# Attention in a three-stage kernel: values projected into token layout for two heads at once, and units written out

## The chip, the cores and the metric

One core of one Trainium2 chip runs the whole kernel. The metric is device time in microseconds (us) of that core, the median of several executions of the same program. TensorE is called PE in the profile, VectorE DVE, ScalarE ACT, GpSimd POOL; SyncE (SP) issues the DMA transfers. A weight load of TensorE has a row of its own there, PEld.

## The reference

The input x has four batches of 512 tokens with 256 features. Three stages follow one another, each adding to x: a mixture-of-experts stage, attention, and the mixture-of-experts stage again. The change touches attention alone:

```python
x = x + attn(layernorm(x))
# in attn: 16 heads of 128 features
q = x @ Wq + bq;  k = x @ Wk + bk;  v = x @ Wv + bv    # W = codes * scales, one scale for 32 rows
scores = einsum('bqhd,bkhd->bhqk', q, k) / sqrt(128)
attn = softmax(scores);  out = einsum('bhqk,bkhd->bqhd', attn, v)
return out.reshape(B, S, 2048) @ Wo + bo
```

## The kernel before

**Precision.** Every large product is made of three matmuls (`mm3`, lines 1006 to 1010): an operand is held as a high part and a low part in fp32r, and high by high, high by low and low by high are added up in PSUM. ACT writes the high part (a copy out of PSUM that rounds), DVE the low part (PSUM minus the high part, the helper `low`, line 1202, or `low_biased`, line 1206).

**Start of attention.** The layernorm (`norm_vector` and its companions, lines 237 to 316) writes the transposed, normalised activations xT (256 features by 2048 tokens, high and low). DVE normalises (line 264), PE transposes (line 301), ACT and DVE copy out (lines 315 and 273). POOL computes one small power for it (line 289) before anything else.

**Weights.** SP loads the codes and scales of one head at a time: for each of q, k and v one transfer of codes (line 963) and two of scales, each row read 32 times (line 968), then one transfer of codes and one of scales for the output projection (lines 970 and 972), 11 transfers and 1 MB in all. POOL multiplies them (line 984), makes the high part (989) and the low part (991) of `w`, which is double buffered by head. The raw buffers are single: SP waits for the low part before it loads the next head. Between the weights of head 0 and of head 1, POOL adds the output bias to x (line 997).

**Units.** A unit is one batch of one head; there are 64, in the order head, batch. For a unit the kernel needs the transposed queries and keys (`queries`, `keys`, lines 1020 and 1029: 6 matmuls of 512 columns each, into the banks b_p 0 and 1), and the values in token layout. The values are projected transposed (`values`, line 1036: again 6 matmuls of 512 columns), ACT adds the bias on the way to `vT` (line 1141), and PE turns `vT` back by four 128x128 transposes (`turn_values`, line 1040, matmuls of line 1044). ACT (line 1147) and DVE (line 1202) split the result into high and low.

**The order of the work** is written out by hand in `step(u)` for each engine (PE at line 1085, ACT at 1169, DVE at 1232). A step has four parts i = 0 to 3. In part i PE turns block i of the unit's probabilities (`turn_probs`, line 1062, four transposes), makes the scores of query block i of the next unit (`scores`), multiplies block i-1 of the turned probabilities by the values (`probs_values`), and does one piece more: in part 0 half of an output projection (`output`, six matmuls of 256 columns) and the queries two units ahead, in part 1 the keys two units ahead, in part 2 the values one unit ahead and the other half of an output projection, in part 3 `turn_values`; `probs_values` of block 3 ends the step. ACT copies each turned block (line 1161) and then runs the exponentials of the next unit's block i (line 1154); DVE writes the low part of the turned block (line 1202) and then the row maxima of the next unit's scores (line 1217), then the low parts and the additions of the output into x (line 1225). The first transposes of a step wait for all four exponentials of its unit:

```python
if kb == 0:
    pe.wait_ge(q["exp_done"], 4 * u + 4)
```

Units 0 to 3 and 60 to 63 are written out; the 56 between them are seven turns of a loop of eight units (`schedule`, line 945), in which waits are against register values. `apart` (line 61) increments a semaphore that nobody waits for, between a wait and an ACT instruction.

Of the kernel before, what the change touches and what calls it, by code (L numbers as in the profile page):

```python
# [25 lines left out]
P = 128  # L26
# [204 lines left out]
def norm_buffers(m):  # L231
    return dict(stats=m.sb("ln_stats", [P, NT, 6]), mean=m.sb("ln_mean", [P, NT]), var=m.sb("ln_var", [P, NT]),
                tmp=m.sb("ln_tmp", [P, NT]), rstd=m.sb("ln_rstd", [P, NT]),
                xn=[m.sb(f"ln_xn{s}", [P, 2, D]) for s in range(2)])
# [671 lines left out]
def attention(nc, c, a, tag):  # L906
# [4 lines left out]
    with ExitStack() as ctx:  # L911
# [9 lines left out]
        vT = m.sb("vT", [P, S])  # L921
        v = [[m.sb(f"v{k}_{s}", [P, 4, HD], F32R) for k in range(2)] for s in range(2)]
# [12 lines left out]
        sems = ("raw_in w_mul w_hi w_ready bo_added s_done nmax_ready exp_done rinv_ready t_done pt_hi pt_lo pv_done "  # L935
                "q_done q_hi q_lo k_done k_hi k_lo vT_done vT_sb v_done v_hi v_lo o_done o_hi o_lo out_done x_added passed")
        q = {n: m.sem(n) for n in sems.split()}
        block = ctx.enter_context(nc.Block())
        LOADS = 11

        def late(t, n):

            return not isinstance(t, int) or t >= n

        def schedule(eng, step):

            for u in range(4):
                step(u, u)
# [3 lines left out]
            for u in range(60, U):  # L952
                step(u, u)

        def later(u, n):

            return not isinstance(u, int) or u + n < U

        @block.sync
        def _(sp):  # L960
            def load(h):
                for n, name in enumerate(("wq", "wk", "wv")):
                    sp.dma_start(raw_c[:, n, :].rearrange("p (c f) -> p c f", c=DC),
                                 a[name + "_codes"].rearrange("(c p) f -> p c f", p=P)[:, :, bass.ds(h * HD, HD)]
                                 ).then_inc(q["raw_in"], 16)
                    for k in range(DC):
                        rows = a[name + "_scales"][k * (P // BLK):(k + 1) * (P // BLK), bass.ds(h * HD, HD)]
                        sp.dma_start(raw_s[:, n, k * HD:(k + 1) * HD],
                                     rows.unsqueeze(1).broadcast_to([P // BLK, BLK, HD])).then_inc(q["raw_in"], 16)
                sp.dma_start(raw_c[:, 3, :], a["wo_codes"][bass.ds(h * HD, HD), :]).then_inc(q["raw_in"], 16)  # L970
                rows = a["wo_scales"][bass.ds(h * (HD // BLK), HD // BLK), :]
                sp.dma_start(raw_s[:, 3, :], rows.unsqueeze(1).broadcast_to([HD // BLK, BLK, D])).then_inc(q["raw_in"], 16)

            load(0)
            with sp.Fori(1, H) as h:
                sp.wait_ge(q["w_ready"], h)
                load(h)

        @block.gpsimd
        def _(pool):  # L980
            def weights(h, s):

                pool.wait_ge(q["raw_in"], 16 * LOADS * (h + 1))
                pool.tensor_tensor(raw_c[:], raw_c[:], raw_s[:], ALU.mult).then_inc(q["w_mul"], 1)
                pool.wait_ge(q["w_mul"], h + 1)
                if late(h, 2):
                    pool.wait_ge(q["out_done"], 2 * B * (h - 1))
                apart(pool, q["passed"])
                pool.tensor_copy(w[s][0][:], raw_c[:]).then_inc(q["w_hi"], 1)  # L989
                pool.wait_ge(q["w_hi"], h + 1)  # L990
                pool.tensor_tensor(w[s][1][:], raw_c[:], f32(w[s][0][:]), ALU.subtract).then_inc(q["w_ready"], 1)
# [7 lines left out]
            weights(1, 1)  # L999
            with pool.Fori(1, H // 2) as k:  # L1000
                for s in range(2):
                    weights(2 * k + s, s)

        @block.tensor
        def _(pe):
# [6 lines left out]
            def project(bank, n, j):  # L1012

                b0, s = (j % 4) * S, (j // 4) % 2
                for d in range(DC):
                    ins = mm3(bank[:], [t[:, n, d * HD:(d + 1) * HD] for t in w[s]], [t[:, d, b0:b0 + S] for t in xT],
                              d == 0, d == DC - 1)
                return ins

            def queries(u, j, hd):  # L1020
                if j % 4 == 0:
                    pe.wait_ge(q["w_ready"], hd + 1)
                if late(u, 2):
                    pe.wait_ge(q["vT_sb"], u - 1)
                elif u == 1:
                    pe.wait_ge(q["q_lo"], 1)
                project(b_p[0], 0, j).then_inc(q["q_done"], 1)

            def keys(u, j):
                if late(u, 2):  # L1030
                    pe.wait_ge(q["v_lo"], u - 1)
                elif u == 1:
                    pe.wait_ge(q["k_lo"], 1)
                project(b_p[1], 1, j).then_inc(q["k_done"], 1)
# [12 lines left out]
            def scores(u, j, i):  # L1047
# [3 lines left out]
                if late(4 * u + i if isinstance(u, int) else u, 2):  # L1051
                    pe.wait_ge(q["exp_done"], 4 * u + i - 1)
                mm3(b_s[i % 2][:], [t[:, i * P:(i + 1) * P] for t in qT[j % 2]], [t[:] for t in kT[j % 2]],
                    True, True).then_inc(q["s_done"], 1)

            def turn_probs(u, j, kb):
                if kb == 0:
                    pe.wait_ge(q["exp_done"], 4 * u + 4)
                if late(4 * u + kb if isinstance(u, int) else u, 2):
                    pe.wait_ge(q["pt_lo"], 4 * u + kb - 1)  # L1060
                for i in range(4):
                    ins = pe.transpose(b_t[kb % 2][:, i * P:(i + 1) * P], pr[j % 2][:, i, kb * P:(kb + 1) * P],  # L1062
# [3 lines left out]
            def probs_values(u, j, kb):  # L1066
                pe.wait_ge(q["pt_lo"], 4 * u + kb + 1)
                if kb == 0:
                    pe.wait_ge(q["v_lo"], u + 1)
                    pe.wait_ge(q["o_lo"], u)  # L1070
                ins = mm3(b_o[:], [t[:, kb, :] for t in v[j % 2]], [t[:] for t in prT[kb % 2]], kb == 0, kb == 3)
                ins.then_inc(q["pv_done"], 1)

            def output(u, j, o):
# [3 lines left out]
                pe.wait_ge(q["x_added"], 2 * u + o)  # L1078
                for t in range(2):
                    i = 2 * o + t  # L1080
                    ins = mm3(b_out[:, t * D:(t + 1) * D], [z[:, i * P:(i + 1) * P] for z in oT[j % 2]],
                              [z[:, 3, :] for z in w[(j // 4) % 2]], True, True)
                ins.then_inc(q["out_done"], 1)

            def step(u, j):
                for i in range(4):
                    turn_probs(u, j, i)
                    if later(u, 1):
                        scores(u + 1, j + 1, i)
                    if i > 0:  # L1090
                        probs_values(u, j, i - 1)
                    if i == 0 and late(u, 2):
                        output(u - 2, j + 6, 1)
                    if i == 0 and later(u, 2):
                        queries(u + 2, j + 2, (u - j) // 4 + (j + 2) // 4)
                    if i == 1 and later(u, 2):
                        keys(u + 2, j + 2)
                    if i == 2 and later(u, 1):
                        values(u + 1, j + 1)
                    if i == 2 and late(u, 1):  # L1100
                        output(u - 1, j + 7, 0)
                    if i == 3 and later(u, 1):
                        turn_values(u + 1)
                probs_values(u, j, 3)
# [11 lines left out]
            output(U - 2, U - 2, 1)  # L1116
# [191 lines left out]
```

## Time and profile before

| | |
|---|---|
| median of 3 runs | 1524.87 us (1523.44 to 1525.94) |
| span of the profiled execution | 1523.9 us |
| attention, first load issued to last unit's work | about 309 to 1240 us |
| PE, weight loads, DVE, ACT, POOL busy in 500 to 640 us, of 140 us | 138.34, 113.01, 94.45, 83.41, 13.39 us |

The profile is of one execution. Its own time is the span, from the first to the last instruction; the median of the runs is 0.97 us above it. A busy time counts an instruction from its start to its modelled end; matmuls overlap, so the distance between the starts of two matmuls is what one costs, and not its duration.

### The profile page before, as it was taken

How to read it: one execution, taken by the hardware profiler on the slowest of the kernel's cores; microseconds unless marked ns; L12 is line 12 of the kernel's file. 1: busy time of each engine (PE TensorE's matmuls, PEld its weight loads, DVE VectorE, ACT ScalarE, POOL GpSimd, SP SyncE). 2: the span in 40 equal slices, each digit the busy share in tenths (PEclk: the TensorE clock that was granted, in tenths of full speed). 3: DMA queues.
4: the chain of work that ended last, by engine and by line, in shares of the span. 5: the costliest groups of instructions: out<-in, count | busy, mean ns of one | idle time of the engine just before them, and what ended most of it. 6: DMA issues, size and time to landing. Idle time of an engine off the chain costs nothing. (4 is left out here: it accounts for less than half of the span.)

```text
span 1523.9 us, 23702 instructions
## 1 busy us (share of the span) xinstructions
PE 1363.6 (89%) x7023; PEld 1086.8 (71%) x7023; DVE 1024.6 (67%) x2366; ACT 700.9 (46%) x1478; POOL 184.2 (12%) x149
## 2 busy tenths in 40 slices
PE   2887799948999999999999999999999948878998
PEld 1666566836878887888788878888888736665677
DVE  4687466865676667666766676667666766874677
ACT  1432352016566556655655565556555523323510
POOL 1111220042010010101001001001000001112200
PEclk7799899959999999999999999999999968988999
DMA  3100671011010011011001001000000000007701
GB/s 124 39 4 7 172 199 29 0 50 33 1 29 23 6 28 28 0 28 28 4 23 28 13 15 28 18 10 28 22 5 0 1 28 31 7 8 192 200 23 37
DMA packets 98147, 58.94 MB, mean 39 GB/s; under 512 B 42032, under 2 KB 97088, under 8 KB 98112
## 3 DMA queue, kind: packets, MB, share of 16 engines
q1 hardware_dynamic: 96576, 53.26, 12.5%
q0 software_dynamic: 1536, 5.24, 1.8%
q8 instruction: 18, 0.29, 0.1%
q14 instruction: 17, 0.14, 0.0%
HBM read 51.13 MB, written 7.36 MB: 38 GB/s over the span
## 5 line engine op out<-in xcount | busy, mean ns | idle before, releaser
L1202 DVE TENSOR_TENSOR at_prT<-at_b_t,at_prT 128x512 fp32r<-128x512 f32 x256 | 177.1, 692 | 239.2 <-ACT at_prT L1161 232.7
L1154 ACT ACTIVATE at_pr<-at_b_s,at_nmax 128x512 f32<-128x512 f32 x256 | 176.1, 688 | 207.1 <-DVE at_junk L1217 199.8
L1161 ACT ACTIVATE at_prT<-at_b_t 128x512 fp32r<-128x512 f32 x256 | 152.9, 597 | 143.4 <-PE at_b_t L1062 143.3
L1217 DVE TENSOR_SCALAR_CACHE_REDUCE at_junk<-at_b_s 128x512 bf16<-128x512 f32 x256 | 174.2, 681 | 1.3 <-PE at_b_s L1010 1.3
L1062 PE MATMUL at_b_t<-keep_ident,at_pr 128*128 128x128 f32 x1024 | 157.1, 276 | 11.6 <-ACT at_pr L1154 7.3
L1062 PEld LDWEIGHTS at_b_t<-keep_ident,at_pr 128*128 128x128 f32 x1024 | 120.0, 140 | 56.8 <-ACT at_pr L1154 34.7
L1008 PE MATMUL at_b_p<-at_xT,at_w 128*128 128x512 f32 x384 | 152.0, 396 | 1.6 <-DVE at_xT L273 1.5
L1010 PE MATMUL at_b_p<-at_xT,at_w 128*128 128x512 f32 x384 | 152.2, 396 | 0.0
L1009 PE MATMUL at_b_p<-at_xT,at_w 128*128 128x512 f32 x384 | 151.5, 395 | 0.0
L1008 PE MATMUL at_b_s<-at_kT,at_qT 128*128 128x512 f32 x256 | 121.8, 476 | 1.4 <-ACT at_pr L1154 1.4
L1225 DVE SCALAR_TENSOR_TENSOR keep_x<-at_b_out,at_rinv,keep_x 128x256 f32<-128x256 f32 x256 | 111.3, 477 | 2.9 <-PE at_b_out L1010 2.9
L1008 PE MATMUL at_b_o<-at_prT,at_v 128*128 128x512 f32 x256 | 106.0, 414 | 1.9 <-DVE at_prT L1202 1.7
L1010 PE MATMUL at_b_s<-at_kT,at_qT 128*128 128x512 f32 x256 | 101.2, 395 | 0.0
L1010 PE MATMUL at_b_o<-at_prT,at_v 128*128 128x512 f32 x256 | 101.0, 394 | 0.0
L1009 PE MATMUL at_b_s<-at_kT,at_qT 128*128 128x512 f32 x256 | 100.7, 393 | 0.0
L1009 PE MATMUL at_b_o<-at_prT,at_v 128*128 128x512 f32 x256 | 100.1, 391 | 0.0
L1010 PEld LDWEIGHTS at_b_p<-at_xT,at_w 128*128 128x128 f32 x384 | 72.5, 189 | 16.5
L1008 PEld LDWEIGHTS at_b_p<-at_xT,at_w 128*128 128x128 f32 x384 | 72.6, 189 | 16.2 <-DVE at_xT L273 1.9
L1009 PEld LDWEIGHTS at_b_p<-at_xT,at_w 128*128 128x128 f32 x384 | 72.6, 189 | 14.2
L989 POOL CAST at_w<-at_raw_c 128x1024 fp32r<-128x1024 f32 x16 | 16.8, 1052 | 490.8 <-PE at_b_out L1010 490.5
L1008 PE MATMUL at_b_out<-at_w,at_oT 128*128 128x256 f32 x256 | 73.1, 285 | 2.5 <-DVE keep_x L1225 2.5
L745 PE MATMUL e_b_act<-e_guT,e_xgT 128*128 128x512 f32 x128 | 65.8, 638 | 8.8 <-DVE e_guT L847 4.0
(192 smaller groups left out, 2905.1 us busy)
## 6 DMA issues: line engine op xcount, KB each, us to landing
e_raw_g<-in_gate_w SPq DMA_DIRECT2D x32, 256.0 KB, 3.7
e_raw_u<-in_up_w SPq DMA_DIRECT2D x32, 256.0 KB, 3.9
e_raw_d<-in_down_w SPq DMA_DIRECT2D x64, 128.0 KB, 3.9
rows<-f_ln_xn SPq DMA_DIRECT2D x16, 256.0 KB, 2.1
keep_x<-in_x SPq DMA_DIRECT2D x1, 2048.0 KB, 11.9
at_raw_c<-in_wq_codes SPq DMA_DIRECT2D x16, 128.0 KB
at_raw_s<-in_wq_scales SPq DMA_DIRECT2D x32, 64.0 KB
at_raw_c<-in_wk_codes SPq DMA_DIRECT2D x16, 128.0 KB
```

What stands on the lines that cost most here:

```text
L745: ins = pe.matmul(b_act[:], xgT[s][:, k, :], guT[s][:, k, :], start=(k == 0), stop=(k == DC - 1))
L989: pool.tensor_copy(w[s][0][:], raw_c[:]).then_inc(q["w_hi"], 1)
L1008: pe.matmul(out, lhs[0], rhs[0], start=first, stop=False)
L1009: pe.matmul(out, lhs[0], rhs[1], start=False, stop=False)
L1010: return pe.matmul(out, lhs[1], rhs[0], start=False, stop=last)
L1062: ins = pe.transpose(b_t[kb % 2][:, i * P:(i + 1) * P], pr[j % 2][:, i, kb * P:(kb + 1) * P], c["ident"][:])
L1154: act.activation(pr[j % 2][:, i, :], b_s[i % 2][:], ACT.Exp, bias=nmax[:, j % 2, i:i + 1], scale=SCALE, accum_out=rsum[:, j % 2, i:i + 1]) ...
L1161: act.activation(prT[kb % 2][0][:], b_t[kb % 2][:], ACT.Copy).then_inc(q["pt_hi"], 1)
L1202: dve.tensor_tensor(dst, bank, f32(hi), ALU.subtract).then_inc(q[done], 1)
L1217: dve.tensor_scalar(junk[i % 2][:], b_s[i % 2][:], -SCALE, None, ALU.mult, ALU.min, accum_out=nmax[:, j % 2, i:i + 1]).then_inc(q["nmax_re ...
L1225: ins = dve.scalar_tensor_tensor(out=xs, in0=b_out[:, t * D:(t + 1) * D], scalar=rinv[:, j % 4, i:i + 1], in1=xs, op0=ALU.mult, op1=ALU.add)
```

## The change

The units are ordered head pair, batch, head: unit u belongs to pair u // 8, batch (u % 8) // 2, head 2 * pair + u % 2. Weights are loaded, multiplied and split per pair of heads in two parts of 1 MB each: q and k of both heads, then v and the output weights of both heads; each is six transfers, and the second waits until POOL has finished the first. The first queries wait for both parts. The output bias is added to x after both parts of pair 0.

The values of two heads are projected straight into token layout, half a batch per unit: the stationary operand is a 128-token block of xT, the moving one the 256 columns of v weights of both heads, so a unit issues 12 matmuls of 256 columns. `vT`, `turn_values`, and ACT's biased copy are gone. DVE adds the bias, spread over the partitions, on the way out of PSUM into `vs` (which is the layernorm's buffer, reused); ACT copies `vs` to the high part; POOL subtracts for the low part, once per unit. All 64 units are written out with constant waits, and `apart` is not called in attention any more.

```diff
-        nb, ns = norm_buffers(m), norm_sems(m)
+        vs = [m.sb(f"vs{s}", [P, 2, 2 * HD]) for s in range(2)]
+        nb, ns = norm_buffers(m, vs), norm_sems(m)
...
-        w = [[m.sb(f"w{k}_{s}", [P, 4, D], F32R) for k in range(2)] for s in range(2)]
+        bvb = [m.sb(f"bvb{s}", [P, 2 * HD]) for s in range(2)]
+        w = [[m.sb(f"w{k}_{s}", [P, 8, D], F32R) for k in range(2)] for s in range(2)]
...
-            with eng.Fori(0, 7) as k:
-                for j in range(4, 12):
-                    step(8 * k + j, j)
...
+            for p in range(PAIRS):
+                if p > 0:
+                    sp.wait_ge(q["w_ready"], 2 * p)
+                load_qk(p)
+                if p > 1:
+                    sp.wait_ge(q["v_sum"], 2 * B * (p - 1))
+                sp.dma_start(bvb[p % 2][:], a["bv"][p * 2 * HD:(p + 1) * 2 * HD].partition_broadcast(P)
+                             ).then_inc(bv_in[p % 2], 16)
+                sp.wait_ge(q["w_ready"], 2 * p + 1)
+                load_vo(p)
...
             norm_pool(pool, c, nb, ns)
-            weights(0, 0)
+            for part in range(2):
+                weights(0, part)
 
             pool.wait_ge(ns["xn_ready"], NT // 2)
             pool.tensor_tensor(c["x"][:], c["x"][:], c["bo"][:].unsqueeze(1).broadcast_to([P, NT, D]),
                                ALU.add).then_inc(q["bo_added"], 1)
...
+            for n in range(U):
+                values(n)
+                if n % (2 * B) in (3, 4) and pair_of(n) + 1 < PAIRS:
+                    weights(pair_of(n) + 1, n % (2 * B) - 3)
...
+            def queries(u):
+                if u % (2 * B) == 0:
+                    pe.wait_ge(q["w_ready"], 2 * pair_of(u) + 2)
+                if u > 0:
+                    pe.wait_ge(q["v_sum"], u)
+                project(b_p[0], 0, u).then_inc(q["q_done"], 1)
...
-            def values(u, j):
-                pe.wait_ge(q["q_lo"], u + 2 if later(u, 1) else U)
-                project(b_p[0], 2, j).then_inc(q["vT_done"], 1)
-
-            def turn_values(u):
-                pe.wait_ge(q["k_lo"], u + 2 if later(u, 1) else U)
-                pe.wait_ge(q["vT_sb"], u + 1)
-                for t in range(4):
-                    ins = pe.transpose(b_p[1][:, t * P:(t + 1) * P], vT[:, t * P:(t + 1) * P], c["ident"][:])
+            def values(n):
+                pe.wait_ge(q["q_lo"], n + 1)
+                for t in range(2):
+                    t0 = batch_of(n) * S + (2 * (n % 2) + t) * P
+                    for d in range(DC):
+                        ins = mm3(b_p[0][:, t * D:(t + 1) * D], [z[:, d, t0:t0 + P] for z in xT],
+                                  [z[:, 4 + d, :] for z in w[pair_of(n) % 2]], d == 0, d == DC - 1)
                 ins.then_inc(q["v_done"], 1)
...
             for u in range(2):
-                queries(u, u, 0)
-                keys(u, u)
-            values(0, 0)
-            turn_values(0)
+                queries(u)
+                keys(u)
+                values(u)
             for i in range(4):
-                scores(0, 0, i)
-            schedule(pe, step)
+                scores(0, i)
+            for u in range(U):
+                for i in range(4):
+                    turn_probs(u, i)
...
+                    if i == 2 and u + 2 < U:
+                        values(u + 2)
+                    if i == 2 and u >= 1:
+                        output(u - 1, 0)
+                probs_values(u, 3)
```

In the steps of the other engines: ACT's copy to the high part stands in part 0 (`values(u + 1)`, where the copy of the turned values stood); DVE's addition stands in part 3, behind the maxima and ahead of the addition of an output into x (`values(u + 2)`, then `add(u - 1, 0)`); DVE's low part of the values in part 0 is gone. On PE `probs_values` waits for POOL's low part of the values at blocks 0 and 2. POOL's own list is `values(n)` for every unit, with the weights of the next pair behind units 3 and 4 of each pair. The pieces of part 3 on PE are now `turn_probs`, `scores`, and `probs_values` of blocks 2 and 3.

## Rows read from the trace of the kernel before

**Rows 1.** Busy time by stretch: PE, weight loads, DVE, ACT, POOL, granted clock, DMA.

```profile
346.00:354.00 8.00, 3.97 (x19) 2.66 (x19) 3.40 (x10) 5.49 (x11) 5.74 (x3) 1.00 0.06 16
500.00:640.00 140.00, 138.34 (x753) 113.01 (x752) 94.45 (x210) 83.41 (x173) 13.39 (x7) 1.00 0.06 15
```

**Rows 2.** Timeline, PE through a unit: start us, us, engine, line, what.

```profile
601.09 0.66 PE L1062 MATMUL at_b_t<-keep_ident,at_pr 128*128 128x128 f32 x4
...
609.41 0.40 PE L1008 MATMUL at_b_p<-at_xT,at_w 128*128 128x512 f32 x1
...
610.81 0.28 PE L1008 MATMUL at_b_out<-at_w,at_oT 128*128 128x256 f32 x1
...
611.51 0.60 PE L1062 MATMUL at_b_t<-keep_ident,at_pr 128*128 128x128 f32 x4
...
613.11 0.40 PE L1010 MATMUL at_b_o<-at_prT,at_v 128*128 128x512 f32 x1
613.47 0.63 PE L1044 MATMUL at_b_p<-keep_ident,at_vT 128*128 128x128 f32 x4
613.86 0.47 PE L1008 MATMUL at_b_o<-at_prT,at_v 128*128 128x512 f32 x1
...
614.95 0.66 PE L1062 MATMUL at_b_t<-keep_ident,at_pr 128*128 128x128 f32 x4 [0.15 <-ACT at_pr L1154]
```

**Rows 3.** Timeline, ACT and DVE around part 3 of the same unit.

```profile
601.69 0.69 DVE L1202 TENSOR_TENSOR at_oT<-at_b_o,at_oT 128x512 fp32r<-128x512 f32 x1 [0.68 <-ACT at_oT L1167]
...
612.15 0.60 ACT L1161 ACTIVATE at_prT<-at_b_t 128x512 fp32r<-128x512 f32 x1 [1.19 <-PE at_b_t L1062]
...
612.78 0.69 DVE L1202 TENSOR_TENSOR at_prT<-at_b_t,at_prT 128x512 fp32r<-128x512 f32 x1 [1.97 <-ACT at_prT L1161]
...
613.39 0.68 DVE L1217 TENSOR_SCALAR_CACHE_REDUCE at_junk<-at_b_s 128x512 bf16<-128x512 f32 x1
...
614.11 0.69 ACT L1154 ACTIVATE at_pr<-at_b_s,at_nmax 128x512 f32<-128x512 f32 x1 [0.79 <-DVE at_junk L1217]
...
614.70 0.19 ACT L1154 ACTIVATION_READ_ACCUMULATOR at_pr<-at_b_s,at_nmax 128x1 f32 x1
```

**Rows 4.** Waits, 360 to 1220 us: engine, what waited, for whom, us, times, longest.

```profile
PEld at_b_t L1062 <- ACT at_pr L1154: 32.1, 55, 0.6
PEld at_b_t L1062 <- issue: 4.6, 7, 0.7
```

**Rows 5.** Timeline, SP, POOL, DVE and PE at the start of attention.

```profile
308.86 0.38 SPq L963 DMA_DIRECT2D at_raw_c<-in_wq_codes  x1
...
312.34 1.22 SPq L963 DMA_DIRECT2D at_raw_c<-in_wv_codes  x1
...
316.12 2.94 POOL L289 TENSOR_TENSOR at_ln_rstd<-at_ln_var,keep_mhalf 128x16 f32<-128x16 f32 x1 [83.38 <-DVE at_ln_var L255]
316.59 1.16 SPq L972 DMA_DIRECT2D at_raw_s<-in_wo_scales  x1
...
322.54 0.72 DVE L264 TENSOR_SCALAR at_ln_xn<-keep_x,at_ln_mean,at_ln_rstd 128x256 f32 x2
...
324.09 2.34 POOL L984 TENSOR_TENSOR at_raw_c<-at_raw_c,at_raw_s 128x1024 f32<-128x1024 f32 x1 [5.03 <-DMA at_raw_s<-in_wo_scales]
...
327.43 2.95 DVE L264 TENSOR_SCALAR at_ln_xn<-keep_x,at_ln_mean,at_ln_rstd 128x256 f32 x2
327.89 2.34 POOL L991 TENSOR_TENSOR at_w<-at_raw_c,at_w 128x1024 fp32r<-128x1024 f32 x1
...
333.29 8.93 POOL L997 TENSOR_TENSOR keep_x<-keep_x,keep_bo 128x4096 f32<-128x4096 f32 x1 [3.06 <-DVE at_ln_xn L264]
...
336.56 0.80 PE L1008 MATMUL at_b_p<-at_xT,at_w 128*128 128x512 f32 x1 [1.51 <-DVE at_xT L273]
...
353.79 0.66 PE L1062 MATMUL at_b_t<-keep_ident,at_pr 128*128 128x128 f32 x4 [1.60 <-ACT at_pr L1154]
```

**Rows 6.** Groups by line and shape: POOL's subtraction of 128x512 in another stage.

```profile
L611 POOL TENSOR_TENSOR f_hT<-f_hid,f_hT 128x512 fp32r<-128x512 f32 x24 | 31.3, 1302 | 188.6 <-ACT f_hT L459 188.6
```

More of the change, by code:

```diff
@@ L937, in attention @@
         q = {n: m.sem(n) for n in sems.split()}
+        bv_in = [m.sem(f"bv_in{s}") for s in range(2)]
         block = ctx.enter_context(nc.Block())
[L939 to L948, printed above, removed]
-            with eng.Fori(0, 7) as k:
-                for j in range(4, 12):
-                    step(8 * k + j, j)
-            for u in range(60, U):
-                step(u, u)
@@ L955, in later, with pair_of, batch_of, head_of @@
-        def later(u, n):
-            return not isinstance(u, int) or u + n < U
+        PAIRS, LOADS = H // 2, 6
+        def pair_of(u):
+            return u // (2 * B)
+        def batch_of(u):
+            return (u % (2 * B)) // 2
+        def head_of(u):
+            return 2 * pair_of(u) + u % 2
         @block.sync
         def _(sp):
[L961 to L964, printed above, removed]
-                                 ).then_inc(q["raw_in"], 16)
[L966 to L977, printed above, removed]
@@ new lines, in _ @@
+            for p in range(PAIRS):
[8 more added lines that the diff above has]
+                load_vo(p)
+            for s in range(2):
+                sp.wait_ge(bv_in[s], 16 * PAIRS // 2)
@@ L1010, in mm3, with project @@
                 return pe.matmul(out, lhs[1], rhs[0], start=False, stop=last)
-            def project(bank, n, j):
-                b0, s = (j % 4) * S, (j // 4) % 2
+            def project(bank, n, u):
+                b0, h = batch_of(u) * S, u % 2
                 for d in range(DC):
-                    ins = mm3(bank[:], [t[:, n, d * HD:(d + 1) * HD] for t in w[s]], [t[:, d, b0:b0 + S] for t in xT],
-                              d == 0, d == DC - 1)
-                return ins
[L1020 to L1027, printed above, removed]
@@ L1083, in output @@
                 ins.then_inc(q["out_done"], 1)
[L1085 to L1104, printed above, removed]
@@ L1117, in _, with queries @@
+            output(U - 2, 1)
             for o in range(2):
-                output(U - 1, U - 1, o)
+                output(U - 1, o)
         @block.scalar
         def _(act):
-            def queries(u, j):
+            def queries(u):
                 act.wait_ge(q["q_done"], u + 1)
-                if late(u, 2):
+                if u >= 2:
                     act.wait_ge(q["s_done"], 4 * (u - 1))
-                apart(act, q["passed"])
-                act.activation(qT[j % 2][0][:], b_p[0][:], ACT.Identity, bias=bias(c["bq"], u, j)).then_inc(q["q_hi"], 1)
@@ L1149, in exps, with values @@
-            def exps(u, j, i):
-                if i == 0 and late(u, 1):
+                if u >= 2:
+                    act.wait_ge(q["s_done"], 4 * (u - 1))
+                h = head_of(u)
+                act.activation(kT[u % 2][0][:], b_p[1][:], ACT.Identity, bias=c["bk"][:, h:h + 1]).then_inc(q["k_hi"], 1)
+            def values(n):
+                g, half = n // 2, n % 2
+                act.wait_ge(q["v_sum"], n + 1)
+                if g >= 2:
+                    act.wait_ge(q["pv_done"], 8 * (g - 1))
+                act.activation(v[g % 2][0][:, 2 * half:2 * half + 2, :].rearrange("p t f -> p (t f)"), vs[half][:].rearrange("p t f -> p (t f)"), ACT.Copy
+                               ).then_inc(q["v_hi"], 1)
@@ L1166, in outputs @@
                     act.wait_ge(q["out_done"], 2 * (u - 1))
-                act.activation(oT[j % 2][0][:], b_o[:], ACT.Copy).then_inc(q["o_hi"], 1)
-            def step(u, j):
-                if late(u, 1):
-                    outputs(u - 1, j + 7)
+                act.activation(oT[u % 2][0][:], b_o[:], ACT.Copy).then_inc(q["o_hi"], 1)
+            norm_scalar(act, nb, ns, xT)
+            for u in range(2):
+                queries(u)
+                keys(u)
+                if u == 1:
+                    values(0)
@@ L1173, in step @@
+            for i in range(4):
+                exps(0, i)
+            for u in range(U):
+                if u >= 1:
+                    outputs(u - 1)
                 for i in range(4):
                     turned_probs(u, i)
-                    if i == 0 and late(u, 1):
-                        turned_values(u, j)
-                    if i == 1 and later(u, 2):
-                        queries(u + 2, j + 2)
-                    if i == 2 and later(u, 2):
-                        keys(u + 2, j + 2)
@@ L1181, in step @@
-                    if i == 3 and later(u, 1):
-                        values(u + 1, j + 1)
-                    if later(u, 1):
-                        exps(u + 1, j + 1, i)
-            norm_scalar(act, nb, ns, xT)
-            for u in range(2):
-                queries(u, u)
-                keys(u, u)
-            values(0, 0)
-            turned_values(0, 0)
-            for i in range(4):
-                exps(0, 0, i)
-            schedule(act, step)
-            outputs(U - 1, U - 1)
+                    if i == 0 and u + 1 < U:
+                        values(u + 1)
@@ L1197, in _ @@
+                    if i == 1 and u + 2 < U:
+                        queries(u + 2)
+                    if i == 2 and u + 2 < U:
+                        keys(u + 2)
+                    if u + 1 < U:
+                        exps(u + 1, i)
+            outputs(U - 1)
         @block.vector
@@ L1232, in step, with outputs @@
-            def step(u, j):
-                if late(u, 1):
-                    outputs(u, j + 7)
+            def outputs(u):
+                low(oT[u % 2][0][:], b_o[:], oT[u % 2][1][:], "o_hi", u + 1, "o_lo")
+            norm_vector(dve, c, nb, ns, xT, False)
+            for u in range(2):
+                low_biased(qT, b_p[0], "q", "bq", u)
+                low_biased(kT, b_p[1], "k", "bk", u)
+                values(u)
+            for i in range(4):
+                maxima(0, i)
+            for u in range(U):
+                if u >= 1:
+                    outputs(u - 1)
@@ L1258, in _ @@
-            norm_vector(dve, c, nb, ns, xT, False)
-            for u in range(2):
-                low_biased(qT, b_p[0], "q", "bq", u, u)
-                low_biased(kT, b_p[1], "k", "bk", u, u)
-            turned_values(0, 0)
-            for i in range(4):
-                maxima(0, 0, i)
-            schedule(dve, step)
-            outputs(U, U - 1)
-            add(U - 2, U - 2, 1)
+                        if u + 2 < U:
+                            low_biased(qT, b_p[0], "q", "bq", u + 2)
@@ L1268, in _ @@
+                        if u >= 2:
+                            add(u - 2, 1)
+                    if i == 2 and u + 2 < U:
+                        low_biased(kT, b_p[1], "k", "bk", u + 2)
+                    if i == 3:
+                        if u + 2 < U:
+                            values(u + 2)
+                        if u >= 1:
+                            add(u - 1, 0)
+            outputs(U - 1)
+            add(U - 2, 1)
             for o in range(2):
-                add(U - 1, U - 1, o)
+                add(U - 1, o)
```

195 lines of the change are left out of this document (107 added, 88 removed).

## The prediction

> **What bounds the kernel now.** I read the busy times by stretch first. In the middle of attention PE is busy for 138.34 of 140 us at full clock, against 94.45 for DVE, 83.41 for ACT and 13.39 for POOL [rows 1]. Read so, anything taken from PE comes off the time, 64 times over. The modelled ends of the matmuls hide short gaps, though, so I read the timeline of one unit next, by starts alone. The unit that begins at 601.09 ends at 614.95, 13.86 us later [rows 2]. Its parts 0 to 2 are back to back on PE: 601.09 to 611.51, 10.42 us. Part 3, from 611.51 to 614.95, is 3.44 us, and here PE is not what ends it. Its last three matmuls begin at 613.86; the first of three behind transposes takes 0.31 (its duration is 0.47 instead of 0.40, so 0.08 more than 0.23), the others 0.23 each, so PE could go on at 614.63. It goes on at 614.95, and the row says behind ACT's exponentials.
>
> So I followed that wait backwards. The turned block leaves PE at 611.51 + 0.60 = 612.11. ACT copies it from 612.15, DVE takes its low part from 612.78, the maxima of the next unit's last score block stand behind that on DVE, from 613.39, the exponentials begin at 614.11, and the read of their sum ends at 614.70 + 0.19 = 614.89 [rows 3]. PE starts 0.06 later. This is an unbroken chain of 3.44 us, which begins with PE's turn in part 3 and ends with PE's turn in part 0. The waits show that it isn't this unit alone: the weight load of `turn_probs` waits 55 times for the exponentials, 32.1 us, 0.58 each, and 7 times, 4.6 us, with "issue" as its reason, 0.66 each; together 62 of 63 steps that have a next unit [rows 4]. A unit is thus 10.42 us of PE work and 3.44 us of latency.
>
> **The change, part by part.**
>
> *The four transposes of `turn_values`.* The matmul before them starts at 613.11 and is done issuing at 613.34; without them the next would start at 613.34, and be 0.23 long instead of 0.31. That is 613.86 - 613.34 + 0.08 = 0.60 us per unit, 38 us over 63 to 64 units, the whole prize. But they stand inside part 3, and none of the chain's links is theirs. `probs_values` of block 3 still waits for DVE's low part, which ends at 612.78 + 0.69 = 613.47, so it moves from 613.86 to about 613.5; then PE waits for 614.95 as before. I cost the removal at nothing. What is late next is the same exponential; the gap on PE grows from about 0.3 to about 0.7 us.
>
> *ACT's and DVE's part in part 3.* ACT's biased copy to `vT` ran while DVE made the low part; the exponentials waited 0.79 us for DVE all the same [rows 3]. Nothing. DVE's new addition of the bias (0.7 us; the low part it replaces cost as much) stands behind the maxima, so behind the chain. It pushes the addition into x from 613.99 to about 614.6, ending near 615.5. Waiting behind it are the low part of oT, which starts at 601.69 + 13.86 = 615.55 today because ACT is late, and PE's next half of `output`, at 1.2 us into the next step, 616.1. Both are met, the first by under 0.1 us. Nothing.
>
> *The projection.* Six matmuls of 512 columns took 610.81 - 609.41 = 1.40 us; six of 256 columns took 611.51 - 610.81 = 0.70 [rows 2], so twelve take 1.41. They stand in part 2, where PE does bound: +0.01 to +0.03 per unit, +1.2 us over 62.
>
> *ACT's copy and POOL's low part.* ACT's copy in part 0 replaces one of the same size. POOL's subtraction costs 1.3 us [rows 6], so about 84 us more on an engine with 13.39 of 140 busy. ACT's copy is over before the first third of the 10.42 us is, so the low part is ready 4.8 us into a step at the latest; block 2 of the values is needed in part 3, more than 10.4 us into it. When POOL makes weights first (6.1 us), the order of its list leaves the low part still ready before that; a load of up to 15 us is hidden too.
>
> *The loop and its registers.* Seven gaps are 0.66 instead of 0.58 [rows 4], so a turn of the loop costs 0.08 us: -0.5 us in all. In the chain PE starts 0.06 after the exponentials inside the loop; register waits add nothing I can see.
> The Trainium skill (Runtime: NRT & Kernel Launch, section "Instruction fetch mechanics") says that straight code is fetched ahead block by block and its cost mostly hidden, and that a taken branch out of the fetched window stalls the engine. By it the long code is free and the loop the dear one; the trace agrees only to the 0.08 us.
>
> *The start.* Here the change adds a wait. The first queries now need both parts of the weights. Before: first transfer issued at 308.86, POOL multiplies at 324.09, 15.2 us for 11 transfers, and the three POOL instructions end at 327.89 + 2.34 = 330.23, 6.1 us after [rows 5]. PE began at 336.56, held by the layernorm, so the weights were hidden. After: the q and k part has six transfers. SP took 312.34 - 308.86 = 3.5 us for its first six, and from its last issue's end (317.75) to POOL's start were 6.3 us, so I take 9.8 us for a load of six. Bounds: 6 us (3.5, and a landing as quick as 2.5, below any tail here) and 15.2 (the same bytes, the same time). Part one lands at 318.7, but POOL is in its power until 316.12 + 2.94 = 319.06. It multiplies at 319.1 and is done at 325.2; only then is part two loaded: 325.2 + 9.8 = 335.0, and 6.1 of POOL make 341.1. PE starts at 341.1 instead of 336.56: +4.6 us, between +0.8 and +10. The bias on x follows, 8.93 us, over by 350; unit 0 needs it only some 20 us after PE starts.
> DVE's normalising took 2.95 us beside POOL's weights and 0.72 without [rows 5]. POOL's first part now stands ahead in that stretch; even were DVE shut out for all of its 6.1 us, instead of the 4.4 lost today (two such, 2.2 each), the layernorm would end by 338.3, ahead of the weights.
> The Trainium skill (SBUF — State Buffer, on the shared port pair) says that DVE and GpSimd lock each other out whole, but not where DVE has one SBUF input and no two-port mode. The rows on the normalising agree with the lock; by it POOL's 64 new subtractions hold up none of DVE's instructions in a step, all of which but one tiny reciprocal read PSUM.
> Between PE's start and the first `turn_probs` lay 17.2 us (336.56 to 353.79). The new order, each bank handed on after its copy out, gives 17.3: +0.1.
>
> *The end.* Step 62 has no values to project (all are one step earlier): its part 2 loses 1.4 us of PE, of which ACT and DVE behind it let through about 1.2: -1.2.
>
> **Sum.** +4.6 + 0.1 + 1.2 - 0.5 - 1.2 = +4.2 us. The profiled execution's span of 1523.9 becomes 1528.1; the median of the runs is 1.0 above the span, so 1529.1.
>
> **The rivals.**
>
> *The removed work counts* (faster). Then 62 x 0.60 = 37 us come off: 1524.9 + 4.2 - 37 = 1492. For it: PE's busy share. Against it: the 62 waits. It would decide if part 3's chain were under 3.44 - 0.6 us after the change, which needs one link gone; I find none that the diff touches.
>
> *Loads are quick* (no change). With 6 us per load PE starts at 337.3 and the sum is +0.4: 1525.3. For it: half the number of rows for the same bytes. Against: six transfers still issue one by one, and the tail of 6.3 us stood behind the last of them.
>
> *Instruction fetch or POOL in the way* (slower still). 64 units of straight code, some 230 PE instructions each. Units 0 to 3, straight already, run at the same pace. Were a boundary as dear as a turn of the loop, 0.08 each, it would be +5 (1534); were it a whole 0.66 outside the gap, +42 (1571).
>
> *A lower clock.* PE idles 0.4 us more per unit. At 346 to 354 PE was busy for 3.97 of 8 us and the granted clock stayed 1.00 [rows 1]. I give it nothing of its own.
>
> **How the numbers follow.** Forecast with its late start 0.72; quick loads 0.10; removed work counts, in full or in part, 0.11; fetch or POOL 0.07. A measurement of this kernel tells 0.2%, 3 us, from no change. From the forecast 0.14 fall within that (a load below 8 us) and 0.58 above; with 0.10 and 0.07: same 0.24, slower 0.65, faster 0.11. The range holds the forecast with start delays of +0.8 to +10 and half a microsecond each way for the steps, and so the quick loads: 1523.5 to 1537. Left out are the 0.11 and most of the 0.07.
>
> **What the profile would show.** Right: a unit of 13.86 us still; `turn_probs` waiting for exponentials 63 times, by the same chain; PE's busy share in the middle down by some 4% with the time unmoved; the second load issued near 325 and PE's first projection near 341. Wrong: a unit of 13.3 us or so, or weights ready by 337. A unit over 13.95 with "issue" or POOL as the reason would speak for the last rival but one.

## The result, and the profile after

The kernel after takes 1535.31 us, the median of 4 runs (1528.33 to 1536.87), against 1525.37 for the kernel before: a ratio of 1.0069, 95% interval 1.004 to 1.0098. A second set on one chip gave 1531.28 (1530.61 to 1535.74, 5 runs) against 1524.54, 1.0045 (1.003 to 1.0059). It is slower, by 7 to 10 us, which is less than 1%.

The runs of one kernel differ by several us, and a part of that lies ahead of the change: POOL's power in the layernorm of attention (line 289) begins between 312.0 and 316.5 us in the profiles of this study, in kernels that are the same up to there. So where profiles are compared I use attention's own span, from that instruction to the next stage's first statistics (line 242): 1238.83 - 316.12 = 922.71 us before, 1248.18 - 316.13 = 932.05 after, 932.67 in the second profile of after. The change costs attention 9.3 to 10.0 us. These are the two ends in the kernel after:

```profile
316.13 2.94 POOL L289 TENSOR_TENSOR at_ln_rstd<-at_ln_var,keep_mhalf 128x16 f32<-128x16 f32 x1 [83.22 <-DVE at_ln_var L255]
...
1248.18 1.41 DVE L242 BATCH_NORM_STATS2 f_ln_stats<-keep_x  x4 [1.31 <-PEq L108]
```

and the second of them in the kernel before:

```profile
1238.83 5.32 DVE L242 BATCH_NORM_STATS2 f_ln_stats<-keep_x  x16 [1.29 <-PEq L108]
```

The busy times of the same stretch as in [rows 1], of the kernel after:

```profile
500.00:640.00 140.00, 135.18 (x767) 111.54 (x766) 95.00 (x214) 76.80 (x161) 37.08 (x23) 1.00 0.09 27
```

PE is down from 138.34 to 135.18 of 140 us, ACT from 83.41 to 76.80, and POOL up from 13.39 to 37.08. The clock is full. The kernel does less on its fullest engine and is no faster: the work came out of a gap.

One unit of the kernel after on PE (`turn_probs` is line 1074 now, the matmuls of `mm3` are 1026 to 1028), to be read against [rows 2]:

```profile
601.93 0.60 PE L1074 MATMUL at_b_t<-keep_ident,at_pr 128*128 128x128 f32 x4
...
603.76 0.28 PE L1026 MATMUL at_b_p<-at_w,at_xT 128*128 128x256 f32 x1
...
605.19 0.28 PE L1026 MATMUL at_b_out<-at_w,at_oT 128*128 128x256 f32 x1
...
605.90 0.60 PE L1074 MATMUL at_b_t<-keep_ident,at_pr 128*128 128x128 f32 x4
...
607.91 0.50 PE L1026 MATMUL at_b_o<-at_prT,at_v 128*128 128x512 f32 x1
...
609.33 0.66 PE L1074 MATMUL at_b_t<-keep_ident,at_pr 128*128 128x128 f32 x4 [0.45 <-ACT at_pr L1160]
```

Part 3, from 605.90 to 609.33, is 3.43 us; it was 3.44. Part 2, from 601.93 to 605.90, is 3.97; it was 3.92, from 607.59 to the 611.51 of [rows 2], by this row of the kernel before:

```profile
607.59 0.60 PE L1062 MATMUL at_b_t<-keep_ident,at_pr 128*128 128x128 f32 x4
```

The twelve projecting matmuls take 605.19 - 603.76 = 1.43 us instead of 1.40. The unit is 13.90 us, 0.04 more. ACT and DVE in part 3, to be read against [rows 3]:

```profile
606.54 0.60 ACT L1167 ACTIVATE at_prT<-at_b_t 128x512 fp32r<-128x512 f32 x1 [1.23 <-PE at_b_t L1074]
...
607.17 0.69 DVE L1203 TENSOR_TENSOR at_prT<-at_b_t,at_prT 128x512 fp32r<-128x512 f32 x1 [2.01 <-ACT at_prT L1167]
...
607.77 0.68 DVE L1226 TENSOR_SCALAR_CACHE_REDUCE at_junk<-at_b_s 128x512 bf16<-128x512 f32 x1
...
608.50 0.69 ACT L1160 ACTIVATE at_pr<-at_b_s,at_nmax 128x512 f32<-128x512 f32 x1 [1.36 <-DVE at_junk L1226]
...
609.09 0.19 ACT L1160 ACTIVATION_READ_ACCUMULATOR at_pr<-at_b_s,at_nmax 128x1 f32 x1
```

Link by link this is the chain of before: copy 0.64 after the transposes began, low part 0.63 later, maxima 0.60, exponentials 0.73, end of the read at 609.28, PE at 609.33. The waits of the kernel after say it over all units, against [rows 4]:

```profile
PEld at_b_t L1074 <- ACT at_pr L1160: 54.9, 62, 0.9
```

All 62 steps in that window wait for the exponentials, 0.89 us each instead of 0.58.

The start, against [rows 5]:

```profile
308.87 0.38 SPq L956 DMA_DIRECT2D at_raw_c<-in_wq_codes  x1
...
320.30 2.40 POOL L996 TENSOR_TENSOR at_raw_c<-at_raw_c,at_raw_s 128x1024 f32<-128x1024 f32 x1 [1.23 <-DMA at_raw_s<-in_wk_scales]
...
326.25 0.37 SPq L956 DMA_DIRECT2D at_raw_c<-in_wv_codes  x1
...
328.37 1.52 SPq L975 DMA_DIRECT2D at_raw_s<-in_wo_scales  x2
...
337.91 2.34 POOL L996 TENSOR_TENSOR at_raw_c<-at_raw_c,at_raw_s 128x1024 f32<-128x1024 f32 x1 [11.68 <-DMA at_raw_s<-in_wo_scales]
...
343.92 0.76 PE L1026 MATMUL at_b_p<-at_xT,at_w 128*128 128x512 f32 x1 [9.72 <-POOL at_w L1002]
...
361.34 0.66 PE L1074 MATMUL at_b_t<-keep_ident,at_pr 128*128 128x128 f32 x4 [1.60 <-ACT at_pr L1160]
```

PE starts at 343.92 instead of 336.56, 7.36 us later, named as POOL's weights; the first load took 11.4 us (308.87 to 320.30), the second 11.7 (326.25 to 337.91).

The last unit but one (step 62) begins in the kernel after with

```profile
1220.89 0.66 PE L1074 MATMUL at_b_t<-keep_ident,at_pr 128*128 128x128 f32 x4 [0.45 <-ACT at_pr L1160]
```

and in the kernel before with

```profile
1210.88 0.66 PE L1062 MATMUL at_b_t<-keep_ident,at_pr 128*128 128x128 f32 x4
```

**Where the 10 us are.** First projection +7.36. From there to the first `turn_probs` 17.42 instead of 17.23, +0.2. From there to step 62 (1220.89 - 361.34 = 859.55 against 1210.88 - 353.79 = 857.09) +2.5. Step 62 -0.1, the last unit up to line 242 15.83 instead of 16.42, -0.6. Together +9.3, attention's difference; the rest of the profiled spans' 10.1 is in the next stage, which the change doesn't touch.

The small terms are no sharper than the profiles. From the first projection to the first `turn_probs` the second profile of the kernel after takes 18.38 us at a mean granted clock of 0.84, the first 17.42 at 0.92. The last unit takes 15.27 and 15.83 us in the two (clock 0.97 and 0.89). The 62 steps between take 859.55 us in the kernel after and 858.64 in one of the experiments below (e4), whose steps are the same. So the start's +7.4 is clear of this, the steps cost 1.5 to 2.5 us, and the +0.2 and the -0.6 can't be told from such differences.

### The profile page after: what moved, and what is told of

The parts are those of the page before. It is cut to its first block and busy times, and to the rows that moved or that the text cites. A ratio compares the mean times of both kernels' runs of the same rounds, so it can differ in the third digit from the quotient of the medians.

```text
span 1534.0 us, 22467 instructions
## 1 busy us (share of the span) xinstructions
PE 1343.5 (88%) x7151; PEld 1078.8 (70%) x7151; DVE 1022.8 (67%) x2366; ACT 659.1 (43%) x1414; POOL 265.8 (17%) x213
## 3 DMA queue, kind: packets, MB, share of 16 engines
HBM read 52.17 MB, written 7.36 MB: 39 GB/s over the span
## 5 line engine op out<-in xcount | busy, mean ns | idle before, releaser
L1008 POOL TENSOR_TENSOR at_v<-at_vs,at_v 128x512 fp32r<-128x512 f32 x64 | 82.3, 1286 | 676.2 <-ACT at_v L1152 676.2
L1074 PE MATMUL at_b_t<-keep_ident,at_pr 128*128 128x128 f32 x1024 | 156.9, 276 | 30.2 <-ACT at_pr L1160 30.2
L1026 PE MATMUL at_b_p<-at_xT,at_w 128*128 128x512 f32 x256 | 101.3, 396 | 10.5 <-POOL at_w L1002 9.7
L1028 PE MATMUL at_b_p<-at_xT,at_w 128*128 128x512 f32 x256 | 101.7, 397 | 0.0
L1027 PE MATMUL at_b_p<-at_xT,at_w 128*128 128x512 f32 x256 | 101.0, 395 | 0.0
L1026 PEld LDWEIGHTS at_b_o<-at_prT,at_v 128*128 128x128 f32 x256 | 48.0, 187 | 39.7 <-DVE at_prT L1203 31.8
L828 DVE TENSOR_TENSOR e_hot<-keep_iota_t,keep_tok 128x2048 fp32r<-128x2048 f32 x32 | 73.0, 2281 | 0.0
L1026 PE MATMUL at_b_p<-at_w,at_xT 128*128 128x256 f32 x256 | 72.3, 283 | 0.3 <-DVE at_qT L1208 0.2
## 6 DMA issues: line engine op xcount, KB each, us to landing
keep_x<-in_x SPq DMA_DIRECT2D x1, 2048.0 KB, 12.6
```

The costliest lines, as they stand in the source:

```text
L828: dve.tensor_tensor(hot[s][:], c["iota_t"][:, bass.ds(i * P, P)].unsqueeze(1).broadcast_to([P, NG, P]), r["tok"][:].unsqueeze(2).broadcast ...
L1008: pool.tensor_tensor(lo, vs[half][:].rearrange("p t f -> p (t f)"), f32(hi), ALU.subtract).then_inc(q["v_lo"], 1)
L1026: pe.matmul(out, lhs[0], rhs[0], start=first, stop=False)
L1027: pe.matmul(out, lhs[0], rhs[1], start=False, stop=False)
L1028: return pe.matmul(out, lhs[1], rhs[0], start=False, stop=last)
L1074: ins = pe.transpose(b_t[kb % 2][:, i * P:(i + 1) * P], pr[u % 2][:, i, kb * P:(kb + 1) * P], c["ident"][:])
```

## The experiments

**One transpose instead of four (e1), and twelve (e2).** Does PE's work in part 3 count? Both kernels are the kernel before with one line changed.

```diff
-                for t in range(4):
+                for t in range(1):
                     ins = pe.transpose(b_p[1][:, t * P:(t + 1) * P], vT[:, t * P:(t + 1) * P], c["ident"][:])
```

> The kernel before with one of the four transposes of turn_values instead of four (three quarters of the values stay unturned, so that part of the computation is left out). Latency theory (part 3 ends with the exponentials, not with PE): nothing moves, the unit stays 13.86 us, the time 1525 us within 2. Rival (PE's work counts): three transposes at 0.09 us come off each of 63 units, 17 us, so about 1508 us and a unit of 13.58.

Measured: 1524.79 us against 1524.12, ratio 1.0 (0.999 to 1.0011), over 10 runs; attention 922.62 us against 922.71. Part 3 of a unit in its profile:

```profile
611.77 0.60 PE L1062 MATMUL at_b_t<-keep_ident,at_pr 128*128 128x128 f32 x4
613.73 0.30 PE L1044 MATMUL at_b_p<-keep_ident,at_vT 128*128 128x128 f32 x1
615.20 0.66 PE L1062 MATMUL at_b_t<-keep_ident,at_pr 128*128 128x128 f32 x4 [0.46 <-ACT at_pr L1154]
```

Part 3 is 3.43 us, as with four; the wait has grown. Nothing of what was removed came off the time.

```diff
-                for t in range(4):
+                for t in 3 * list(range(4)):
```

> The kernel before with the four transposes of turn_values issued three times over. Latency theory: of the added 8 x 0.09 = 0.75 us the gap of 0.32 us swallows its part, so +0.43 us per unit, 27 us, about 1552 us, and the gap ahead of the first transposes is gone. Rival (PE's work counts in full): +47 us, 1572 us.

Measured: 1555.13 us, ratio 1.0202 (1.0185 to 1.0219), +31 us; attention 953.82, +31.1. Part 3 of a unit on PE, with twelve transposes:

```profile
604.97 0.60 PE L1062 MATMUL at_b_t<-keep_ident,at_pr 128*128 128x128 f32 x4
606.93 1.50 PE L1044 MATMUL at_b_p<-keep_ident,at_vT 128*128 128x128 f32 x12
608.95 0.60 PE L1062 MATMUL at_b_t<-keep_ident,at_pr 128*128 128x128 f32 x4
```

Part 3 is 3.98 us and ends without a wait: +0.54. The gap swallowed the first 0.3 of some 0.86 added (eight at 0.108; I had 0.09), so the slack was real and as small as the trace had it. Part 0, which no longer begins behind a wait, is 3.22 us instead of 3.29, so a unit grows by 0.49, and 62 of them make 30.2 of the 31.1 us. Together with e1: removed work gives nothing, added work counts beyond the gap.

**Filling the gap (e5 in the kernel after, e6 in the kernel before).** If part 3 waits, work moved into it from a part that PE bounds should come off the time, and more so in the kernel after, whose gap is wider.

```diff
-                    if i == 2 and u >= 1:
+                    if i == 3 and u >= 1:
                         output(u - 1, 0)
```

> The kernel after with the six matmuls of the first half of the output projection moved from part 2 to part 3, where PE waits. Latency theory: part 3 stays 3.43 us (PE's work in it grows from about 2.6 to 3.3), part 2 loses 0.70, a unit is 13.20 instead of 13.90, 44 us less over 63 units: about 1491 us. Rival (the order on PE doesn't matter since its sum bounds the unit): 1535 us as the kernel after.

> The kernel before with the same move. Latency theory: PE's work in part 3 becomes 3.84 us, over the chain's 3.44, so only the gap of 0.3 is won: a unit of 13.56, 19 us less, about 1506 us. The difference to the kernel after with the same move is then what the removed transposes and copies are worth once PE is what ends part 3: some 15 us. Rival: 1525 us.

Measured: the kernel after with the move 1488.00 us, ratio 0.9761 (0.9744 to 0.9777); the kernel before with it (there `output` follows `turn_values`) 1503.48, 0.9852 (0.9833 to 0.9871). In attention's span 885.24 and 901.16: 46.8 and 21.5 us less than each without the move. The kernel after with the move:

```profile
603.23 0.60 PE L1074 MATMUL at_b_t<-keep_ident,at_pr 128*128 128x128 f32 x4
606.66 0.66 PE L1074 MATMUL at_b_t<-keep_ident,at_pr 128*128 128x128 f32 x4
...
616.39 0.60 PE L1074 MATMUL at_b_t<-keep_ident,at_pr 128*128 128x128 f32 x4
619.82 0.66 PE L1074 MATMUL at_b_t<-keep_ident,at_pr 128*128 128x128 f32 x4
```

The kernel before with it:

```profile
604.86 0.60 PE L1062 MATMUL at_b_t<-keep_ident,at_pr 128*128 128x128 f32 x4
606.81 0.63 PE L1044 MATMUL at_b_p<-keep_ident,at_vT 128*128 128x128 f32 x4
607.20 0.36 PE L1008 MATMUL at_b_out<-at_w,at_oT 128*128 128x256 f32 x1
...
608.69 0.60 PE L1062 MATMUL at_b_t<-keep_ident,at_pr 128*128 128x128 f32 x4
```

In the first, part 3 is 3.43 us with six matmuls more in it, the chain's length still, and the unit 13.16; the weight load still waits for the exponentials at the end of it, 63 times, 0.47 us each. In the second it is 3.83, PE's work, and the units are 13.49 to 13.53. Over the 62 steps the kernel after takes 815.4 us and the kernel before 835.4: with this move the change is worth 0.32 us per unit, 19.9 us, against the nothing that it gave in a wait. Of these 5.3 go to the later start; in the times, with what the end gives back, 15.5 remain. The change was not useless; its gain was left in a wait.

**The loop (e3).** The kernel before with `schedule` reduced to constants, and nothing else.

```diff
-            for u in range(4):
-                step(u, u)
-            with eng.Fori(0, 7) as k:
-                for j in range(4, 12):
-                    step(8 * k + j, j)
-            for u in range(60, U):
+            for u in range(U):
                 step(u, u)
```

> The kernel before with its 64 units written out with constant waits, and nothing else. By the trace of before, seven turns of the loop at 0.08 us go: -0.5 us, not to be told from 1524.5. Rival (straight code costs through instruction fetch, and that is part of the 10 us): +3 us or more, with waits named issue.

Measured: 1525.14 us, ratio 1.0002 (0.9991 to 1.0014); attention 922.28 us, 0.43 less than before. Neither a gain to measure nor a cost of straight code. The 0.43 is a sum of parts that go both ways: the 62 steps take 856.55 us instead of 857.09, which fits the 0.5 but is less than the 0.9 by which equal steps differed above; from the first projection to the first `turn_probs` it is 18.24 us instead of 17.23, at a mean granted clock of 0.83 instead of 0.90.

**The start.** Three kernels, each the kernel after with part of the late start undone: the wait split (e4), a second buffer for the loads (e7), and both with POOL held back (e10).

```diff
                 if u % (2 * B) == 0:
-                    pe.wait_ge(q["w_ready"], 2 * pair_of(u) + 2)
+                    pe.wait_ge(q["w_ready"], 2 * pair_of(u) + (1 if u == 0 else 2))
...
             def values(n):
                 pe.wait_ge(q["q_lo"], n + 1)
+                if n == 0:
+                    pe.wait_ge(q["w_ready"], 2)
```

> The kernel after, where the first queries and keys wait only for the first part of the weights, and the first values for the second. Theory (7.4 of the 10 us are PE's later start behind the second load): PE's first projection near 336.5 instead of 343.9, but the first values still at 343.8 instead of 348.4, so -4.6 us against the kernel after. Rival (the later start is caught up in the steps): no change.

Measured, beside the kernel after repeated:

> The kernel after, unchanged, to stand beside the next three on one chip. 1535 us if the first result's profiled execution is typical, 10 us over the kernel before; 1528 to 1530 if its one quick run was.

The kernel after 1531.28 us; with the split wait 1529.57 (1.0032, 1.0019 to 1.0045); attention 928.20, 3.9 less than in the first profile of the kernel after and 4.5 less than in the second (932.67). The medians differ by 1.7 us, and their intervals overlap, so it is the profiles that show it. PE's first projection comes 20.2 us after POOL's power, as in the kernel before (20.4).

The second load at once, into the probabilities' buffer, which is idle until the first exponentials, with a semaphore of its own:

```diff
+        first_c, first_s = (pr[0][:, 2 * k:2 * k + 2, :].rearrange("p a (b d) -> p (a b) d", d=D) for k in range(2))
...
-                sp.wait_ge(q["w_ready"], 2 * p + 1)
+                if p > 0:
+                    sp.wait_ge(q["w_ready"], 2 * p + 1)
                 load_vo(p)
...
+                if n == 1:
+                    pool.wait_ge(q["first_in"], 16 * LOADS)
```

> The kernel after, where the second part of the first pair's weights is loaded at once into a buffer that is still idle, behind the first part instead of after POOL's work on it. Theory: the second part lands near 331, POOL is ready near 337, PE starts near 337 instead of 343.9: -6.9 us against the kernel after. Rival (the two loads share the same few DMA engines and the second lands no earlier than 338): no change.

Measured: 1530.13 us (1.0038, 1.0025 to 1.0051); attention 928.64, 3.4 to 4.0 less instead of 6.9; the medians again differ by less than their intervals. My mechanism was wrong in one link, and the profile of this kernel shows which, first on DVE in the layernorm:

```profile
321.01 3.00 DVE L264 TENSOR_SCALAR at_vs<-keep_x,at_ln_mean,at_ln_rstd 128x256 f32 x2
...
324.54 2.85 DVE L264 TENSOR_SCALAR at_vs<-keep_x,at_ln_mean,at_ln_rstd 128x256 f32 x2
...
327.91 3.00 DVE L264 TENSOR_SCALAR at_vs<-keep_x,at_ln_mean,at_ln_rstd 128x256 f32 x2
...
331.43 0.72 DVE L264 TENSOR_SCALAR at_vs<-keep_x,at_ln_mean,at_ln_rstd 128x256 f32 x2
```

In the same kernel, POOL's two of the second part and PE's first matmul in the same stretch:

```profile
324.89 2.34 POOL L1003 TENSOR_TENSOR at_pr<-at_pr 128x1024 f32<-128x1024 f32 x1 [1.02 <-DMA at_pr<-in_wo_scales]
...
328.42 2.34 POOL L1009 TENSOR_TENSOR at_w<-at_pr,at_w 128x1024 fp32r<-128x1024 f32 x1
...
337.09 0.80 PE L1033 MATMUL at_b_p<-at_xT,at_w 128*128 128x512 f32 x1 [1.51 <-DVE at_xT L273]
```

The second part landed early, and POOL was done with it at 330.76, 18.2 us after its power. But now POOL's work covered most of the layernorm, DVE's normalising took near 3 us four times over instead of 0.72, and PE waited for the layernorm until 24.5 us after the power. The next kernel is built against that: as e7, with the split wait of e4 and POOL's second part held back.

```diff
                 if n == 1:
+                    pool.wait_ge(ns["xn_ready"], NT // 2)
                     pool.wait_ge(q["first_in"], 16 * LOADS)
```

> The kernel after with the idle buffer for the second load, with the first queries waiting for the first part alone, and with POOL's work on the second part held back until DVE has normalised all of x. Theory (the start costs 7.4 us, and the buffer alone won only 3.3 because POOL's 12 us of weights then shut DVE out of the layernorm): DVE loses only what it lost in the kernel before, PE starts 20.4 us after POOL's power as before, the second part is ready 23 us after it, ahead of the first values at 25; attention, from POOL's power to the next stage's first statistics, 925 us instead of 932, the time 1528. Rival (the lock isn't what held the layernorm): PE starts no earlier than 24 us after the power, attention 928.5 or more.

Measured: 1526.90 us, ratio 1.0008 (0.9997 to 1.0019); attention 924.66. POOL at the start of this kernel, the power and then the second part of the weights:

```profile
314.63 2.94 POOL L289 TENSOR_TENSOR at_ln_rstd<-at_ln_var,keep_mhalf 128x16 f32<-128x16 f32 x1 [83.14 <-DVE at_ln_var L255]
...
331.81 2.35 POOL L1004 TENSOR_TENSOR at_pr<-at_pr 128x1024 f32<-128x1024 f32 x1 [8.07 <-DVE at_vs L264]
...
335.35 2.37 POOL L1010 TENSOR_TENSOR at_w<-at_pr,at_w 128x1024 fp32r<-128x1024 f32 x1
```

And the first projecting matmul of the same kernel on PE:

```profile
335.08 0.80 PE L1034 MATMUL at_b_p<-at_xT,at_w 128*128 128x512 f32 x1 [1.51 <-DVE at_xT L273]
```

PE starts 20.45 us after the power, and 7.4 of the 9.3 us are gone. The 2.0 that stay are the steps', less the end (+2.5 - 0.6). Here the time itself shows it: the ratio's interval lies below that of the kernel after, 1.003 to 1.0059.

**The two together (e9)**, e10's start and the output in part 3:

> The same start, and the first half of the output projection in part 3. The two are apart in time, so they add up: attention about 880 us, the time about 1482 us, 42 below the kernel before. Rival (PE's fuller part 3 gives the start's gain back): 1488 us.

Measured: 1482.82 us (1480.14 to 1485.37), ratio 0.9727 (0.9711 to 0.9743), attention 879.64. This beats both kernels, the one before by 42 us.

## Why the prediction was right, and where it was off

- *The removal of the four transposes is worth nothing.* Right: part 3 3.43 us, the unit 13.90, 62 waits for the same chain, and shown by e1 and e2 apart from the rest of the change. The gap grew from 0.58 to 0.89 on the weight load's row. PE's busy share fell by 2.3% (138.34 to 135.18), where I had said some 4: some of the new idle time lies ahead of `probs_values` of block 3, where PE begins at 607.91, 0.42 us after the matmul before it (607.49) instead of 0.23, and the modelled ends cover it.
- *DVE's addition, ACT's copy, POOL's subtraction in the steps: nothing.* Right as far as the trace shows: DVE's instructions kept their lengths (0.69, 0.68), and the steps' +2.5 is used up by part 2 on PE (62 times 0.05, less the loop's 0.5). POOL's 64 subtractions were not tried by themselves.
- *The twelve matmuls of 256 columns, +1.2, the loop -0.5.* The projection costs 0.03 us more and part 2 0.05, so +2.5 net, where I had +0.7; this is read from the traces, and no kernel tried the twelve matmuls by themselves. For the loop, e3 agrees with -0.5 and can't tell it from nothing.
- *The start, +4.6.* The mechanism was right, and the size is the term that was mis-sized: +7.4. I had put a load of six transfers at 9.8 us from six issues and the tail behind the last; the second took 11.7, because its tail was 8.0 us (329.89 to 337.91) and not 6.3. That is 1.9 of the 2.8 us that were missing. The first load took 11.4 and so landed at 320.30, 1.2 after POOL's power, where I had it hidden; POOL and PE gave back the rest. The bound of +10 took that in, but it was worked out with only the second load slow: with 15.2 us for both, the first would have landed at 324.1 and the bound would have been +15. In the profiles with this wait the second load took 11.1 to 13.0 us (e5 and the kernel after again), so the size of this term isn't fixed either.
- *The layernorm isn't held up further by POOL.* In the kernel after that held: DVE's last piece of it ended at 335.65, ahead of the weights (343.78). In e7's expectation I forgot my own row on it: 12 us of POOL's weights over the normalising moved PE's start by 4 us.
- *The end, -1.2.* Step 62 lost its values and gave 0.1, not 1.2: its part 3 grew from 3.43 to 4.41, since DVE and ACT were now behind (PE waits 0.99 us in it for DVE's low part). The other 0.6 is the last unit's, and e3, with the work of the kernel before, has the same (15.79 us instead of 16.42, granted clock 1.00 instead of 0.86).
- Sum: +4.2 predicted, +10.1 in the profiled execution, of which 0.7 outside attention; in the range of 1523.5 to 1537 both times. There is luck in the first of the two: the bounds named in the prediction give 1529.1 + 5.4 + 0.5 = 1535.0 at most, and 1535.31 lies in the 2 us more that the range has without a term for it. The steps cost 1.5 to 2.5 us instead of 0.7, which is outside the half microsecond that I had allowed them.

The rival that the removed work counts fell with e1. The rival of quick loads fell too: they were slower than taken. A dear instruction fetch fell with e3. The lower clock fell for the steps with the 1.00 of the stretch; at the start the clock was below full in both kernels (0.90 and 0.92 up to the first `turn_probs`), and a lower one went with up to 1 us more from profile to profile, before and after alike.

## What to carry to other kernels

An engine that is busy for 98% may still not be what ends a step; read the starts through one period, find where it resumes behind a wait, and ask whether the removed work stands before or inside that wait. Work taken out of a wait is worth nothing until other work is moved into its place: here one moved call turned 10 us of loss into 36 us of gain, of which the same call gives 21 without the change. And a wait that is hidden at steady state is paid at the start, where two loads through one buffer stood in series ahead of the first matmul.

## What the runs showed of the hardware

- DVE's normalising of 128x256 from SBUF to SBUF, two at a time, took 0.72 to 0.74 us alone and 2.23 to 3.00 beside POOL's weights; DVE's instructions that read PSUM kept 0.69 and 0.68 beside POOL. In e7 the slowed pairs end 0.15 to 0.16 us after the POOL instruction beside them (327.39 after 327.23, 330.91 after 330.76). The Trainium skill (SBUF — State Buffer, section "Who interferes with whom") has it as an exclusive lock; e7 and e10 agree, with 4 us at stake from the place of POOL's work alone.
- Two loads of six transfers issued in a row overlap, but only in part: in e7 the first 1 MB was taken up by POOL 12.6 us after the first issue (305.30 to 317.87) and the second 19.6 us after it (324.89). In the kernel after, one behind the other, the second was taken up after 29.0 us (308.87 to 337.91), 5.95 of them POOL's work on the first.
- A turn of the loop on PE, ACT and DVE, with waits against registers, cost PE 0.08 us (0.66 instead of 0.58 ahead of the first transposes); 64 units of straight code cost nothing that could be measured (ratio 1.0002 in e3).
- Matmuls of 512 columns in the first projections of the kernel after stood 0.43 us apart while the granted clock was at its lower level, 0.50 (344.48 to 344.91), and 0.23 us apart at 1.00 (346.96 to 347.19).
